# Causal attention for 192 heads on one core: row maxima over up to 1024 columns at once, their row sent by a DMA, the key-side mask as one GpSimd select

## The reference

```
k = (x @ Wk).reshape(B, H, T, hs)
q = (x @ Wq).reshape(B, H, T, hs)
v = (x @ Wv).reshape(B, H, T, hs)
wei = jnp.einsum('bhtd,bhsd->bhts', q, k) * scale
mask = jnp.tril(jnp.ones((T, T), dtype=bool))
wei = jnp.where(mask, wei, -jnp.inf)
wei = jax.nn.softmax(wei, axis=-1)
out = jnp.einsum('bhts,bhsd->bhtd', wei, v).reshape(B, T, C)
```

## Time and profile before

| | |
|---|---|
| median of three runs | 3497.25 us (3497.21 to 3500.66) |
| the profiled execution | 3498.39 us, span 3496.7 us |
| PE, DVE, ACT, POOL busy over the span | 92%, 69%, 59%, 22% |
| mean granted TensorE clock | 0.968 |
| attention, 1150 to 2840 us | 1690 us, granted clock 1.00 |
| what is ahead of it and behind it | the first block, to about 1095 us; the feed-forward part, from about 2850 us |

### The profile page before, as it was taken

The page is one execution under the profiler, slowest core; times in us unless marked ns, Lnnn a source line. Parts: engine busy times, 40 slices in busy tenths (PEclk is TensorE's granted clock), DMA queues, the critical chain, the costliest instruction groups (busy, mean ns, idle before and its releaser), DMA issues. The chain is left out here.

```text
span 3496.7 us, 85276 instructions
## 1 busy us (share of the span) xinstructions
PE 3229.6 (92%) x28894; PEld 1775.0 (51%) x28894; DVE 2397.6 (69%) x4745; ACT 2069.6 (59%) x3730; POOL 766.1 (22%) x1529
## 2 busy tenths in 40 slices
PE   4999999999985999999999999999999989988896
PEld 2444545445542555555555555555555544443442
DVE  4566566566654777777777777777777755656665
ACT  2677777777753555555555555555555546555554
POOL 0233444444444122121221212212122100000000
PEclk8999999999997999999999999999999989989998
DMA  1122222222224555545455455554555531211221
GB/s 28 37 77 95 94 78 81 94 94 94 95 77 126 99 92 93 97 89 97 93 93 97 89 97 93 93 97 89 97 93 93 97 67 45 82 45 39 78 72 45
DMA packets 889092, 291.02 MB, mean 83 GB/s; under 512 B 840625, under 2 KB 873682, under 8 KB 889042
## 3 DMA queue, kind: packets, MB, share of 16 engines
q1 hardware_dynamic: 889042, 290.37, 37.5%
HBM read 101.55 MB, written 88.08 MB: 54 GB/s over the span
## 5 line engine op out<-in xcount | busy, mean ns | idle before, releaser
L906 ACT ACTIVATE at_probs<-at_ps_keys 128x512 f32<-128x512 f32 x1728 | 992.8, 600 | 738.7 <-PE at_ps_keys L838 616.4
L924 DVE TENSOR_REDUCE at_unit_max<-at_ps_queries 128x1 f32<-128x512 f32 (+3 forms) x2304 | 1153.7, 551 | 196.0 <-PE at_ps_queries L824 164.3
L824 PE MATMUL at_ps_queries<-at_turned 96*128 96x512 bf16 (+3 forms) x2304 | 681.5, 332 | 61.2 <-DMA at_turned<-at_spread 31.1
L838 PE MATMUL at_ps_keys<-at_turned 128*128 128x128 bf16 (+3 forms) x3456 | 660.5, 273 | 2.1 <-ACT at_probs L906 1.4
L857 PE MATMUL at_ps_values<-at_probs,at_v 128*32 128x128 f32 x13824 | 497.1, 277 | 0.1
L857 PEld LDWEIGHTS at_ps_values<-at_probs,at_v 128*32 128x32 f32 x13824 | 342.2, 109 | 134.8 <-ACT at_probs L906 68.6
L784 POOL TENSOR_TENSOR at_v<-at_stacks,at_one 128x128 f32<-128x128 f32 x192 | 77.0, 401 | 1383.6 <-PE at_ps_values L857 1341.7
L838 PEld LDWEIGHTS at_ps_keys<-at_turned 128*128 128x128 bf16 x3456 | 255.5, 97 | 223.9 <-issue 80.2
L824 PEld LDWEIGHTS at_ps_queries<-at_turned 96*128 96x128 bf16 x2304 | 191.7, 97 | 315.1 <-DVE at_unit_max L924 224.9
L827 PE MATMUL at_ps_queries<-mask_queries,ident_bf 128*128 128x128 bf16 x1536 | 330.3, 221 | 0.0
L650 PE MATMUL cb_ps_qkv<-w_attn,cb_x 96*128 96x384 f32 x512 | 198.2, 512 | 5.8 <-ACT cb_a_squares L568 4.3
(11 more groups left out here) (201 smaller groups left out, 4656.4 us busy)
## 6 DMA issues: line engine op xcount, KB each, us to landing
qkv_rows<-cb_packed SPq DMA_DIRECT2D x32, 1536.0 KB, 8.1
at_stacks<-qkv_rows SPq DMA_DIRECT2D x192, 256.0 KB, 3.3
cb_x<-in_x_dram SPq DMA_DIRECT2D x32, 384.0 KB, 3.7
cb_x_again<-in_x_dram SPq DMA_DIRECT2D x32, 384.0 KB, 4.4
x_after_conv<-cb_x SPq DMA_DIRECT2D x32, 384.0 KB, 5.0
attention_rows<-at_att SPq DMA_DIRECT2D x384, 32.0 KB, 2.2
ff_att_rows<-attention_rows SPq DMA_DIRECT2D x32, 384.0 KB, 4.0
ff_x<-x_after_conv SPq DMA_DIRECT2D x32, 384.0 KB, 4.7
```

Source lines behind the costliest of these rows:

```text
L824: mm = pe.matmul(pq[:, u % QBANKS, 0:n], QT[0:STACK, slot, qb * P:(qb + 1) * P], KT[0:STACK, slot, k0:k0 + n], start=True, stop=True)
L838: mm = pe.matmul(pk[:, bank_k, c0:c0 + n * P], KT[:, slot, kb * P:(kb + 1) * P], QT[:, slot, q0 * P:(q0 + n) * P], start=(c0 == 0), stop=True,
L906: act.activation(PR[:, slot_unit % RING, :], pk[:, slot_unit % KBANKS, :], ACT.Exp, scale=scale).then_inc(S["probs"], 1)
L924: dve.tensor_reduce(MX[:, r % 2, qb, k0 // BANK:k0 // BANK + 1], pq[:, u % QBANKS, 0:n], AX.X, ALU.max).then_inc(S["unit_max"], 1)
```

## The change

- The query side goes by whole rows of tiles, longest first (`QROWS`): eight pieces of up to 1024 columns in four PSUM banks. DVE reduces each by one instruction straight to the negated maximum; the reduce of partial maxima is gone. `QFREE` says how many rows must be reduced before PE writes a bank again.
- The two parts of the maxima are 16 columns of one 128x128 tile, turned by one transpose. ACT copies the 16x128 result to `MT`, and a DMA issued by ACT lays it as two rows of 1024 behind the queries. Key unit 0 waits for that DMA (`max_in`).
- `LAG` is 8, so that key unit 0 comes at step 8, five steps after the turn. The pipeline is two heads deeper, and the loop holds six heads.
- The key-side mask products are gone. GpSimd sets the masked probabilities of a head's two diagonal units to 0 after exp, by one `affine_select` over 1024 columns; these units have buffers of their own (`DP`), and the values take them last.
- Values have one bank instead of two; ACT copies their result at step 3, and the output turn is at step 6.

```diff
-    w["mask_keys"] = sb("mask_keys", [P, P], BF16)
...
-    QUNITS = [(qb, k0, min(BANK, (qb + 1) * P - k0)) for qb in range(TILES)
-              for k0 in range(0, (qb + 1) * P, BANK)]
-    NQ = len(QUNITS)
-    SLOTS = 4
-    RING = 6
+    DIAG = 2
+    RING = NU - DIAG
+    SLOTS = 6
     BATCH_UNITS = 3
-    QBANKS, KBANKS = 3, 2
-    LAG = 4
-    VALUES_LAG = LAG + 2
-    MAX_TURN, OUT_TURN = 3, 8
+    KBANKS = 2
+    QBANKS = 4
+    QROWS = [(7, 0), (6, 2), (5, 0), (4, 2), (3, 0), (2, 1), (1, 2), (0, 3)]
+    QFREE = [-2, 0, 1, 2, 3, 3, 4, 4]
+    QSTEP = [0, 1, 2, 3, 5, 6, 7, 8]
+    LAG = 8
+    VALUES_LAG = LAG + 4
+    MAX_TURN, MAX_COPY, MAX_SEND = 3, 3, 4
+    OUT_COPY, OUT_TURN = 3, 6
+    OUT_QROW = 6
...
+                    if on(4):
+                        slot = (r - 4) % SLOTS
+                        pool.wait_ge(S["probs"], NU * (i - 4) + DIAG)
+                        pool.tensor_tensor(TICK[:, slot % 2:slot % 2 + 1], ONE[:, :, 0], ONE[:, :, 0], ALU.mult)
+                        blocks = DP[:, slot % 2, :, :].rearrange("p u (t n) -> p (u t) n", n=P)
+                        pool.affine_select(out=blocks, in_=blocks, compare_op=ALU.is_ge, fill=0.0, base=0,
+                                           pattern=[[0, TILES], [1, P]], channel_multiplier=-1
+                                           ).then_inc(S["masked"], 1)
...
-                    for t in range(TILES):
-                        mm = pe.transpose(turned[96:128, t * P:(t + 1) * P], MP[:, t, :], w["ident_bf"][:, :])
-                    mm.then_inc(S["max_turned"], 1)
+                    _above(pe.wait_ge, S["out_ready"], h - 2)
+                    pe.transpose(max_ps[:, :], MP[:, slot % 2, :], w["ident_bf"][:, :]
+                                 ).then_inc(S["max_turned"], 1)
...
+                    _above(pe.wait_ge, S["row_max"], NQ * h + QFREE[u])
+                    n = (qb + 1) * P
+                    for k0 in range(0, n, BANK):
+                        m = min(BANK, n - k0)
+                        pe.matmul(pq[:, b0 * BANK + k0:b0 * BANK + k0 + m], QT[0:STACK, slot, qb * P:n],
+                                  KT[0:STACK, slot, k0:k0 + m], start=True, stop=True)
...
-                        pe.wait_ge(S["max_ready"], h + 1)
+                        pe.wait_ge(max_in[slot], lands)
...
-                    if UNITS[u][0][0] == UNITS[u][0][1]:
-                        mm = pe.matmul(pk[:, bank_k, :].rearrange("p (t n) -> p t n", n=P), w["ident_bf"][:, :],
-                                       _bcast(w["mask_keys"][:, :], 1, HALF), start=False, stop=True,
-                                       skip_group_check=True)
...
+                        if u == MAX_COPY and on(3):
+                            act.wait_ge(S["max_turned"], i - 2)
+                            _above(act.wait_ge, max_in[(r - 5) % SLOTS], _dmas(lap, r, 5, SLOTS))
+                            act.activation(MT[:, (r - 3) % 2, :], max_ps[0:2 * TILES, :], ACT.Copy
+                                           ).then_inc(S["max_copied"], 1)
+                        if u == MAX_SEND and on(3):
+                            q = (r - 3) % SLOTS
+                            act.wait_ge(S["max_copied"], i - 2)
+                            act.dma_start(QT[STACK:STACK + 2, q, :], MT[:, q % 2, :]).then_inc(max_in[q], 16)
...
-                            dve.wait_ge(S["max_turned"], i - 2)
-                            dve.tensor_copy(QT[96:128, (r - 3) % SLOTS, :], turned[96:128, :]
-                                            ).then_inc(S["max_ready"], 1)
...
+                            dve.tensor_reduce(NM[:, r % 2, qb:qb + 1], pq[:, b0 * BANK:b0 * BANK + (qb + 1) * P], AX.X,
+                                              ALU.max, negate=True).then_inc(S["row_max"], 1)
```

More of the change, by code:

```diff
@@ L725, in causal_attention @@
         AT = sb("att", [P, SLOTS, TILES, HD])
-        pq = pb("queries", [P, QBANKS, BANK])
+        pq = pb("queries", [P, QBANKS * BANK])
         pk = pb("keys", [P, KBANKS, BANK])
-        pv = pb("values", [P, 2, BANK])
+        pv = pb("values", [P, 2 * P])
         bank = pb("turn", [P, BANK])
-        turned = bank[:, :].bitcast(BF16)
-        out_t = [pv[:, i, 0:2 * P] for i in range(2)]
+        max_ps = bank[:, 2 * P:2 * P + P // 2].bitcast(BF16)
         out_ps = bank[:, 0:2 * P].rearrange("p (t d) -> p t d", d=VW)
@@ L898, in body @@
                     for u in range(NU):
-                        back = 3 if u >= LAG else 4
+                        back, k = 3 - (u - LAG) // NU, (u - LAG) % NU
                         if on(back):
-                            v = (u - LAG) % NU
-                            act.wait_ge(S["k_scores"], NU * (i - back) + v + 1)
-                            _above(act.wait_ge, S["values"], NU * (i - back) + v - RING + 1)
-                            slot_unit = (r - back) % SLOTS * NU + v
-                            act.activation(PR[:, slot_unit % RING, :], pk[:, slot_unit % KBANKS, :], ACT.Exp,
-                                           scale=scale).then_inc(S["probs"], 1)
@@ L908, in body @@
-                        if u == OUT_TURN - 2 and on(4):
-                            act.wait_ge(S["values"], NU * (i - 3))
-                            act.activation(OT[:, :], out_t[r % 2], ACT.Copy).then_inc(S["out_copied"], 1)
-                _pipeline(act, body, NHEADS, 5, SLOTS)
+                            h, slot = i - back, (r - back) % SLOTS
+                            act.wait_ge(S["k_scores"], NU * h + k + 1)
+                            if k < DIAG:
+                                if k == 0:
+                                    _above(act.wait_ge, S["values"], NU * (h - 1))
+                                probs = DP[:, slot % 2, k, :]
+                            else:
+                                _above(act.wait_ge, S["values"], NU * (h - 1) + k - DIAG + 1)
+                                probs = PR[:, k - DIAG, :]
@@ new lines, in body @@
+                        if u == MAX_SEND and on(3):
+                            q = (r - 3) % SLOTS
+                            act.wait_ge(S["max_copied"], i - 2)
+                            act.dma_start(QT[STACK:STACK + 2, q, :], MT[:, q % 2, :]).then_inc(max_in[q], 16)
+                        if u == OUT_COPY and on(5):
+                            act.wait_ge(S["values"], NU * (i - 4))
+                            act.activation(OT[:, :], pv[:, :], ACT.Copy).then_inc(S["out_copied"], 1)
```

158 lines of the change are left out of this document (70 added, 88 removed).

## The result

The changed kernel takes 3557.24 us (median, 3553.64 to 3562.72) against 3497.23 us: a ratio of 1.0172, interval [1.0154, 1.019]. It is 60 us slower. The forecast was 3386 us, 110 us faster.

The account below looks back on a forecast made before the run. Attention was taken as bound by PE's own work plus short waits on DVE and ACT. Period 9.10 to 8.40 + 0.09 saves 0.61 us x 192 heads = 117 us: 3498.4 - 117 + 5 = 3386 us; range 3345 to 3560.

Parts of the forecast that it names:

- the row's latency: Attention, DMA of the row of maxima issued by ACT: lands 2.2 us after its issue, taken from 32 KB stores.
- the two ends: Bounds given for the landing time of the row of maxima after its issue: 1.8 and 3.3 us.
- rival 1: Key unit 0 waits for the DMA of maxima, late beside SP's transfers: period 9.14 to 9.34, 3511 to 3550 us; chance 0.22.
- period L + 1.03: Attention, per head: if the row of maxima lands at L, later than 7.2 us, the period is L + 1.03 us.
- The layout of the head: Hand timeline of one attention head from row 7: period 8.22 us with waits of 1.27, if the row lands by 7.2.
- PE's work: Attention, per head: falls 0.79 us to 6.97, of it 0.43 from the two key-mask products removed.
- The select: GpSimd's mask of 128x1024 after exp, per head: takes 1.2 us and is hidden.
- DVE's 1024-column reduce: Attention, DVE's reduce of query row 7: 1.22 us in the hand timeline, from 0.69 to 1.91.
- ACT's issue: DMA of maxima sent by ACT: passes ahead of exp 5, giving L = 7.25 and period 8.3 us; otherwise 9.05.
- rival 2: ACT's DMA issue waits for SP's transpose issue of 3.02 us: period 11.6, about 4000 us; chance 0.12.
- Rival 3: Long rows and ACT's copies stall PE more than laid out: period 8.7 to 8.9, 3430 to 3465 us; chance 0.16.
- The fill of 5 us: Start and end of attention: later keys and a later last output cost some 5 us.

Follow-up runs that it names:

- e2: Changed kernel with SP issuing its next load only once the row of maxima has landed: 3425.37 us, ratio 0.9796 to the kernel before.
- e3: Changed kernel with SP's transpose moved behind the stores and a wait for the row of maxima, load still ahead: 3477.14 us, ratio 0.9951.
- e12: Changed kernel with SP's load halved: first 128 KB ahead of the row of maxima, the second only once it has landed: 3423.1 us.
- e9: Changed kernel with SP's transpose (behind a 256 B DMA) ahead of the row of maxima and the load 2.0 us behind it: 3528.69 us, ratio 1.0088.
- e7: Changed kernel with turn and copy of the maxima at step 2, send at 3 (one step earlier): 3425.28 us, ratio 0.9799.
- e1: Changed kernel with turn and copy of the maxima at step 1, send at 2 (two steps earlier): 3386.84 us, ratio 0.9687.
- e5: e1 with PE's third and fourth query rows a step later (steps 3 and 4): 3315.25 us, ratio 0.9481.
- e10: e5 with the last four query rows at steps 6, 7, 8, 8 and turn, copy and send at 2, 2, 3: 3304.44 us, ratio 0.9448.

## Why the prediction was wrong

**The step that failed** is the row's latency: "I take 2.2, the smallest transfer." Its own latency alone is even below that, 1.78 us (e2). But beside SP's load and transpose it is 3.04 us, near the upper of the two ends, 3.3. The earlier trace rows held both. The stores' 2.2 was chosen by size. It should have been chosen by place: the prediction had itself computed that the load goes out at 4.9, the row at 5.05 and the transpose at 5.4. That the stores still land in 2.2 behind the transpose was the argument against rival 1, and it doesn't carry over. SP can issue them only when its transpose issue of 3 us is over, so they follow the start of it by 3.3 us (2000.66 to 2003.95 in before). The row goes out within 0.2 us of it. The sum's own rule, period L + 1.03, was right: with L = 5.07 + 3.04 = 8.11 and the loop's 0.09 it gives 9.23, and 9.32 was measured. That 3557.24 lies inside the stated 3345 to 3560 is owed to rival 1, which that range takes in; the forecast's own was 3350 to 3430.

**Rival 1** was the case, with mechanism, place and price: key unit 0 waits for the row, whose landing takes 3 us, and the period is 9.32 against "9.14 to 9.34". Its 3511 to 3550 us fall 7 us short of 3557.24. The Trainium skill, "DMA: Bandwidth & Descriptors", Queues, rings and completion order, says that a DMA's semaphore write lands only after every earlier write of that DMA engine across its queues. The runs with a load ahead agree with it: the row lands in 2.62 us where the load lands in 2.69 (e3), in 1.96 where half of it lands in 1.98 (e12), and 0.87 us after its last packet in the changed kernel. What e9 shows is a delay of another kind, of the packets themselves. Rival 1 had 0.22 and deserved more.

**The layout of the head** had a second, smaller error. With the row in time, the same order has a period of 8.70 (e2), not 8.49. Zero is row 7; the measured head is the one shown above, and key 0 is e2's.

| step | laid out | measured |
|---|---|---|
| stall of row 5 for DVE | 0.63 | 0.66 |
| turn of the maxima | 3.34 | 3.48 |
| key 6 | 4.86 | 4.95 |
| send of the row | 5.05 | 5.07 |
| values behind key 6 | 5.07 | 5.45 |
| key 0, if the row is there | 7.22 | 7.55 |

Up to the send it holds to 0.15 us. Then the values come 0.38 late. The first batch of a head also waits for the copy of the previous output out of the single bank of values (L920), which the layout had only on ACT. In e7 the trace names it:

```profile
2003.20 0.38 ACT L920 ACTIVATE at_out_t<-at_ps_values 128x256 f32<-128x256 f32 x1
...
2003.73 0.86 PE L867 MATMUL at_ps_values<-at_probs,at_v 128*32 128x128 f32 x24 [0.16 <-ACT at_out_t L920]
```

From two banks of values to one was a line of the change, and its wait was nowhere in the sum. In the changed kernel, e1, e2 and e7 alike the values start 0.14 to 0.15 us after that copy's end in every head between 1500 and 1900 us. e1 and e7 show what it is worth. They agree up to key 6; then in e7 the DMA's issue stands between exp 4 and the copy, in e1 nothing does, and e1's values start 0.20 us earlier, which is the whole difference of their periods (8.70 - 8.49). Two banks with this order were not tried. What the wait and the rest of the layout missed is 0.21 us a head, about 40 us.

**The sum, term by term.** From 3386 to 3557 are 171 us. The late row makes 0.62 us x 180 heads = 112 us and 18 us of the fill (8th head at 1216.69 against 1198.52 in e2), the lower clock there included; the missed wait and its like about 40.

**What held.** PE's work fell: 83% busy in place of 98%. The select takes 1.09 us (forecast 1.2) and is hidden. Its removal of PE's products was sized at 0.43 us a head as work and is worth 0.26 as time. DVE's 1024-column reduce takes 1.23 us and its row of 128 0.28 as laid out (1.22, 0.286). ACT's issue goes out ahead of exp 5, as taken, and doesn't wait for SP's, so rival 2 was not the case: it lasts 0.63 us, not 1 to 3. The Trainium skill, "Perfetto Trace Analysis", DMA Instruction — HWDGE (DVE, Sync), says that the generator of descriptors is shared, and locked for exclusive use until a DMA's descriptors are all made. No such wait shows in ACT's issue: it starts 0.56 us behind a transpose issue of 3.14 us in the fill and lasts 0.62, and in e9 0.13 us behind one of 1.54 and lasts 0.63. Only the first one of the fill takes 1.46. Whether SP waits for ACT is open: the transpose's issue, 0.17 us behind ACT's, lasts 3.31 us (median) in the changed kernel and 3.04 in e2. The clock in the steady part stayed at 1.00. Rival 3's stalls are real (e5), but they weren't the cause. The fill of 5 us is 4 us in e1; in the changed kernel it is 27, again for the row.

## What to carry to other kernels

A small DMA on which an engine waits is priced by what other queues issue in the microsecond around it, and not by its size alone; place it ahead of the large transfers, or hold those back until it has landed. The order of two issues 0.3 us apart can decide the sign of a whole change. Where a large change costs little or even loses, move its one new wait before judging its parts: here three step numbers turned 1.7% slower into 3.1% faster, two more entries of a step table made that 5.2% (e5), and a wider spread of the rows 5.5% (e10). In a layout by hand, go through every wait in the code for each engine, the buffer counts that the change lowers above all.
